# A two-layer adaLN/FFN kernel: the second layer's split weights stored by column group, with groups of 384, 384 and 288 columns

## What is computed

```python
W = weights[condition]                      # layer 0: a 64x64 mix per batch entry
x0 = einsum('bct,bcd->bdt', x, W)
base_out = x_flat @ W_base.T + b_base       # plus 8 gated experts of rank 16
out = base_out + expert_out                 # x = x + out

result = einsum('bsd,od->bso', x, base_weight) + base_bias   # layer 1, 1024 -> 1024
h = einsum('bsd,brd->bsr', x, lora_A_w[adapter_ids])         # rank 16, one adapter per batch entry
result = result + einsum('bsr,bor->bso', h, lora_B_w[adapter_ids])
x_q = _quant_fp8(x, 1.0 / input_scale)                       # then an fp8-rounded 1024 -> 1024 product
acc = einsum('ni,io->no', x_q, w_q)
out = acc * (input_scale * weight_scale) + bias              # x = x + out
```

## Time and profile before

| | |
|---|---|
| median of 3 runs | 1982.33 us (1981.93 to 1985.19) |
| the profiled execution | 1983.52 us |
| its span, first to last instruction | 1981.7 us |
| around the span | 1.8 us |
| TensorE busy (matmuls) | 1965.5 us, 99% of the span |
| weight loads busy | 1807.6 us, 91% |
| VectorE / ScalarE / GpSimd busy | 75% / 20% / 25% |
| granted TensorE clock | 1.00 |

### The profile page before, as it was taken

One profiled execution on the slowest core, in us unless ns is written; L12 is line 12 of the kernel. 1 busy time (PEld: TensorE's weight loads), 2 busy tenths in 40 slices (PEclk: granted clock), 3 DMA queues, 4 the chain that ended last, 5 costly groups with the idle time before them and its releaser, 6 DMA issues.

```text
span 1981.7 us, 37775 instructions
## 1 busy us (share of the span) xinstructions
PE 1965.5 (99%) x13056; PEld 1807.6 (91%) x13056; DVE 1489.1 (75%) x3874; ACT 400.9 (20%) x1091; POOL 499.6 (25%) x470
## 2 busy tenths in 40 slices
PE   7999999999999999999999999999999999999999
PEld 7999999999999999999998888888888888888887
DVE  7676666687777777766677777777777777777777
ACT  4111111111121212111122212222122211222111
POOL 1444433301111011011022222222222222222222
PEclk9999999999999999999999999999999999999999
DMA  6675444344334433433365555555555555555553
GB/s 215 179 217 177 124 145 126 105 121 121 109 106 121 125 106 106 132 106 98 115 178 172 155 167 158 156 172 152 167 158 156 172 152 167 158 157 170 153 168 114
DMA packets 220678, 290.16 MB, mean 146 GB/s; under 512 B 98118, under 2 KB 169800, under 8 KB 220620
## 3 DMA queue, kind: packets, MB, share of 16 engines
q1 hardware_dynamic: 220620, 289.57, 49.2%
HBM read 163.63 MB, written 109.06 MB: 138 GB/s over the span
## 4 chain that ended last, share of the span: by engine, by line
PE 95%; SPq 1%; DMA 1%; DVE 1%; issue 1%; POOL 1%; ACT 0%; DVEq 0%; POOLq 0%
PE bank_g L1096 14%; PE bank_g L1098 13%; PE bank_g L1097 13%; PE bank_g L1160 12%; PE bank_g L1159 12%; PE bank_g L1158 11%; PE bank_y L1171 11%; PE bank_y L1076 3%; PE bank_g L1126 2%; PE bank_g L1128 2%; PE bank_g L1127 2%; PE bank_g L1204 1%; SPq L488 0%; POOL obuf L659 0%; DMA raw<-a_split 0%
## 5 line engine op out<-in xcount | busy, mean ns | idle before, releaser
L1096 PE MATMUL bank_g<-w0h,st_h 128*128 128x384 f32 (+1 forms) x1536 | 524.9, 342 | 3.3 <-DVE st_l L813 2.2
L1098 PE MATMUL bank_g<-w0h,st_l 128*128 128x384 f32 (+1 forms) x1536 | 520.6, 339 | 0.0
L1097 PE MATMUL bank_g<-w0l,st_h 128*128 128x384 f32 (+1 forms) x1536 | 520.5, 339 | 0.0
L1158 PE MATMUL bank_g<-w1h,st_h 128*128 128x352 f32 x1536 | 505.2, 329 | 0.0
L1160 PE MATMUL bank_g<-w1h,st_l 128*128 128x352 f32 x1536 | 496.1, 323 | 0.0
L1159 PE MATMUL bank_g<-w1l,st_h 128*128 128x352 f32 x1536 | 495.1, 322 | 0.0
L1096 PEld LDWEIGHTS bank_g<-w0h,st_h 128*128 128x128 f32 x1536 | 289.0, 188 | 18.1 <-issue 13.1
L1158 PEld LDWEIGHTS bank_g<-w1h,st_h 128*128 128x128 f32 x1536 | 288.6, 188 | 7.3
L1159 PEld LDWEIGHTS bank_g<-w1l,st_h 128*128 128x128 f32 x1536 | 288.5, 188 | 1.6
L600 POOL TENSOR_TENSOR ring<-ring,b_base_sb 128x1024 f32<-128x1024 f32 x63 | 150.2, 2398 | 553.4 <-PE bank_y L1076 513.3
L1098 PEld LDWEIGHTS bank_g<-w0h,st_l 128*128 128x128 f32 x1536 | 289.2, 188 | 0.0
(11 more groups left out here) (81 smaller groups left out, 1986.6 us busy)
## 6 DMA issues: line engine op xcount, KB each, us to landing
ring<-x SPq DMA_DIRECT2D x64, 512.0 KB, 4.4
x_scratch<-ring SPq DMA_DIRECT2D x64, 512.0 KB, 2.7
x1t_scratch<-x_blocks SPq DMA_DIRECT2D x256, 128.0 KB, 2.5
ring<-x1t_scratch SPq DMA_DIRECT2D x64, 512.0 KB, 3.9
ring<-x_scratch SPq DMA_DIRECT2D x64, 512.0 KB, 3.3
out<-obuf SPq DMA_DIRECT2D x63, 512.0 KB, 2.9
b_stack<-b_split SPq DMA_DIRECT2D x384, 64.0 KB, 2.5
raw<-a_split SPq DMA_DIRECT2D x128, 128.0 KB, 3.0
```

The costliest lines, as they stand in the source:

```text
L1096: pe.matmul(to, st_h[:, rows], w0h[:, k, cols], start=(k == 0), stop=False)
L1097: pe.matmul(to, st_h[:, rows], w0l[:, k, cols], start=False, stop=False)
L1098: last = pe.matmul(to, st_l[:, rows], w0h[:, k, cols], start=False, stop=(k == KC - 1))
L1158: pe.matmul(to, st_h[:, rows], w1h_k[:, k, cols], start=(k == 0), stop=False)
```

## The change

The columns of the three groups become 32 + 352, 384 and 288 (384, 384 and 288 with the slot columns). `w1h` and `w1l` keep their size, but are now three blocks, one for each group, and in a block the eight rows of that group stand one behind the other: rows of 384 columns (1536 bytes), 384 columns and 288 columns (1152 bytes). Everything that names such columns follows: the places of GpSimd's pieces, the slot columns, the matmuls, and through `G1_BASE` and `G1_COL` the evacuations and `add_lora`.

```diff
-G1_BASE = (320, 352, 352)
-G1_COL = (0, 320, 672)
-G1_AT = tuple(LR + c for c in G1_COL)
-W1_COLS = LR + D
+G1_BASE = (352, 384, 288)
+G1_COL = (0, 352, 736)
+G1_SLOT = (LR, 0, 0)
+G1_ROW = tuple(s + n for s, n in zip(G1_SLOT, G1_BASE))
+G1_BLOCK = (0, KC * G1_ROW[0], KC * (G1_ROW[0] + G1_ROW[1]))
+W1_SIZE = KC * sum(G1_ROW)
...
-        w1h = sb("w1h", [P, KC * W1_COLS], F32R)
-        w1l = sb("w1l", [P, KC * W1_COLS], F32R)
-        w1h_k = w1h[:, :].rearrange("p (k n) -> p k n", k=KC)
-        w1l_k = w1l[:, :].rearrange("p (k n) -> p k n", k=KC)
+        w1h = sb("w1h", [P, W1_SIZE], F32R)
+        w1l = sb("w1l", [P, W1_SIZE], F32R)
+
+        def w1_cols(g, k):
+            first = G1_BLOCK[g] + k * G1_ROW[g]
+            return slice(first, first + G1_ROW[g])
...
-                    cols = slice(G1_AT[v], G1_AT[v] + G1_BASE[v])
+                    row = w1_cols(v, u)
+                    cols = slice(row.start + G1_SLOT[v], row.stop)
                     src = w1t[u * P:(u + 1) * P, G1_COL[v]:G1_COL[v] + G1_BASE[v]]
-                    return src, G1_BASE[v], w1h_k[:, u, cols], w1l_k[:, u, cols], None
+                    return src, G1_BASE[v], w1h[:, cols], w1l[:, cols], None
...
-                    for s, w in enumerate((w1h_k, w1l_k)):
-                        to = w[:, :, 0:LR].rearrange("p k (j r) -> p j k r", j=PER_TILE)
+                    for s, w in enumerate((w1h, w1l)):
+                        rows = w[:, 0:G1_BLOCK[1]].rearrange("p (k n) -> p k n", k=KC)
+                        to = rows[:, :, 0:LR].rearrange("p k (j r) -> p j k r", j=PER_TILE)
...
-                    cols = slice(G1_AT[g] - (LR if g == 0 else 0), G1_AT[g] + G1_BASE[g])
-                    to = bank_g[:, g, 0:cols.stop - cols.start]
+                    to = bank_g[:, g, 0:G1_ROW[g]]
...
-                        rows = slice(k * P, (k + 1) * P)
-                        pe.matmul(to, st_h[:, rows], w1h_k[:, k, cols], start=(k == 0), stop=False)
-                        pe.matmul(to, st_h[:, rows], w1l_k[:, k, cols], start=False, stop=False)
-                        last = pe.matmul(to, st_l[:, rows], w1h_k[:, k, cols], start=False, stop=(k == KC - 1))
+                        rows, cols = slice(k * P, (k + 1) * P), w1_cols(g, k)
+                        pe.matmul(to, st_h[:, rows], w1h[:, cols], start=(k == 0), stop=False)
+                        pe.matmul(to, st_h[:, rows], w1l[:, cols], start=False, stop=False)
+                        last = pe.matmul(to, st_l[:, rows], w1h[:, cols], start=False, stop=(k == KC - 1))
```

## The result

| | before | after |
|---|---|---|
| median | 1982.33 us (1981.93 to 1986.0, 5 runs) | 1990.95 us (1990.01 to 1991.48, 5 runs) |
| the profiled execution | 1983.52 us | 1990.16 us |
| its span | 1981.7 us | 1988.4 us |

The ratio is 1.0039, 95% interval 1.0028 to 1.005: the change makes the kernel 8.6 us slower. I had forecast no change.

A forecast was written before the change was run, and what follows sets the result against it. TensorE's own matmul stream was taken as the bound. All terms were 0 except +0.3 us in the last tile, so 1982.3 + 0.3 = 1982.6 us, with a range of 1974 to 1991 us.

The forecast's parts named there:

- signs of being wrong: Wide group at 4.20 us or more, or 4.09; group 2 at 3.84; new waits; time moving over 4 us.
- What bounds the kernel: Layer 1: only TensorE's own stream sets the time, priced by the distance between matmul starts; TensorE busy 99%.
- Step 1, the matmuls: `bank` matmuls in layer 1: column sum stays 1056, fixed part per matmul stays, 11520 ns a tile, change 0.
- the 11.5 ns of layer 1: Fixed part of a layer 1 matmul beyond 0.422 ns a column, read at 352 columns, assumed for 384 and 288.
- the upper bound of 8.7 us: Most that layer 1's matmuls could lose: 5.2 us for the 384-column ones plus 3.5 us for the 288-column ones.
- Steps 2 to 4: Layer 1 work waiting on group ends (0.32 us shifts, covered), evacuations and `add_lora`, layer 0 filling of `w1h`, `w1l`: 0.
- Step 5, the last tile: Last tile: the wait for `ht` goes, but `add_lora` comes 0.2 us later and evacuations are wider: +0.3 us.
- The slower one: Layer 1's 384-column matmuls pay the higher fixed part of layer 0's: 5.2 to 8.7 us slower, chance 0.24.
- The faster rival: Groups 0 and 1: rows 1536 bytes apart, one fixed position modulo 512, stream better: up to 10 us, chance 0.26.
- The weight load as a bound: Group 2: weight loads might keep 288-column matmuls at 160 ns, costing 41 us, 2024 us; chance 0.02.
- The rule on separate read ports: TensorE in layer 1: weight loads take nothing from a running matmul, so no `w1h` layout matters, change 0.
- The uneven 0.47 and 0.49 us: Times of three successive matmuls inside a layer 1 group before the change; basis for a gain of at most 10 us.

The follow-up runs named there:

- e2: Changed kernel with the new widths 384, 384 and 288 but the old rows of 1056 columns (4224 bytes): 1981.93 us, ratio 0.9993 to before.
- e5: Changed kernel with groups 0 and 2 sharing rows of 672 columns, group 1 still a block with rows 1536 bytes apart: 1985.33 us, one run.
- e9: Changed kernel with a gap of 128 bytes between the blocks of groups 0 and 1: 1987.09 us, ratio 1.0019 to before.
- e11: Changed kernel with a gap of 128 bytes behind row 0 of group 0: 1983.36 us, ratio 1.0003 to before.
- e10: Changed kernel with a gap of 256 bytes between the blocks of groups 0 and 1: 1990.32 us, one run.
- e4: Changed kernel with `st_h`, `st_l` and all behind them moved 64 bytes against `w1h` and `w1l`: 1989.4 us, one run.

## Why the prediction was right or wrong

The range held the time, at its upper edge, but the forecast of no change failed, and with it the mechanism behind it. Two of the prediction's own signs of being wrong came: the time moved by more than 4 us, and a wide group took 4.24 us where it had 4.16.

1. *What bounds the kernel*: right. TensorE's stream, and nothing else, moved; there is no new wait.
2. *Step 1, the matmuls*: this is the step that failed, where it takes the 11.5 ns of layer 1 for both new widths because "`w1` rows that start at a multiple of 128 bytes from its beginning, before and after". Multiples of 128 were the wrong thing to look at. The old rows step by 128 over a multiple of 512, the new ones by 0. The fixed part became 14.7 ns in the 3072 wide matmuls, 3.2 ns x 3072 = 9.8 us, and 10.6 in the 1536 narrow ones, -0.9 ns x 1536 = -1.4 us: 8.4 us, against the 8.1 us from the tiles. The narrow price was over by 0.9 ns, so narrow matmuls gave a little back. That the upper bound of 8.7 us held is partly luck: it was 5.2 us for the wide and 3.5 us for the narrow matmuls, and the errors of the two, 4.6 us too little and 4.9 us too much, cancel.
3. *Steps 2 to 4*: right. `ht` and `st_l` are never waited for, evacuations and filling cost nothing that shows.
4. *Step 5, the last tile*: right in kind. The wait for `ht` is gone and one of 0.5 us for the turned `rq` stands in its place. From the start of the last tile's group 0 to the end of the span it is 23.6 us against 23.4, where I had 0.3 more.
5. *The rivals.* The slower one named a price that fits, 5.2 to 8.7 us, for the wrong reason: it took the prices of layer 0's wide matmuls as those of the width or the operands, and e2 shows 384 columns of `w1h` and `w1l` to be free. The faster rival named the right object, a fixed position modulo 512 bytes in place of four in turn, and said that it may as well be the bad one. The time went that way, but the position is not bad by itself: e5, e9, e11 and tiles 0 and 1 of the changed kernel are quick at a fixed position. What counts is the rhythm in which the stream arrives there. The weight load as a bound is out: group 2 follows at 132 ns.
6. *The rule on separate read ports* (the Trainium skill, "TensorE: Matmul & The Clock Gate", section "What happens when you issue a matmul"): had I gone by it, no layout could have mattered, and that would have been wrong by the whole 8 us. Whether the ports are what interferes, no run shows. In the Trainium skill, same page, section "Back-to-back issue gap", the distance is N / 2.4 + 2.5 ns for a matmul alone, 162.5 ns at 384 columns. The traces have 173.3 to 176.7 for fp32r with a new weight load each; 10.8 to 14.2 ns lie on top of it, and the 3.4 ns between the two are decided by the layout and by what runs ahead of the tile.

The uneven 0.47 and 0.49 us that I had read in the earlier trace rows were the sign of all this. I used them as a bound, but did not ask what would become of them when all steps are equal.

## What to carry to other kernels

In a dense stream of matmuls with a weight load each, the distance from one to the next can follow a rhythm of several matmuls, and the rhythm can lock. Here the stream kept whatever rhythm it started in, slow or quick, when all steps of the moving operand were multiples of 512 bytes. When a new layout makes every row start alike modulo 512, look at the distances from start to start, in ns and in order, before and after; a pad of 128 bytes in one place was worth 3 ns on each of some 3000 matmuls here. Change the width of groups and their layout in separate steps: here each was free alone, and only both together cost 0.4%.

## What was not expected of the hardware

- A matmul's distance depends on the history of the stream. Group 1 with the same columns, the same weights and the same layout runs at 176.7 ns (changed kernel from tile 2 on, e10) or at 173.2 to 173.3 (e9, e11), by one step of 128 bytes, in e11 21 matmuls ahead of the group. Within the changed kernel it runs at 173.3 ns in tiles 0 and 1 and at 176.7 behind an `ffn`. Either rhythm holds through a whole group and into the next.
- A step of 128 bytes moves it, one of 256 does not, and a shift of 64 bytes between `st_h`, `st_l`, all behind them and the columns makes another pattern (e4: 175, 174, 174, 175, 182 ns).
- The fixed part over 0.422 ns a column is not one number: 11.3 ns at 384 columns in the quick rhythm (e2), 11.5 at 352, 10.6 at 288 and 14.5 at 480.
- What in the chip makes the rhythm is open. The runs show that it hangs on the steps between the columns of one matmul and the next, and on what ran before; e4 makes the place of the loaded operands against the moving ones likely as well. No run here separates the reading of the columns from that of the weights.
